# Causal row sums: added up on GpSimd over the key tiles, in place of float32r pairs of transposed probabilities

## The chip, the core and the metric

The kernel runs on one core of a Trainium2 chip, in one launch. A core has five engines with queues of their own: TensorE (PE in the profile; its weight loads are PEld), VectorE (DVE), ScalarE (ACT), GpSimd (POOL) and SyncE (SP), which here issues all DMAs. Each executes its queue strictly in order, and they wait for each other by semaphores. The metric is the device time of one execution in microseconds, the median over runs. Lower is better.

## The reference, cut to what matters

Four attention layers follow each other on an image of shape (4, 256, 32, 32): a batch of 4, C = 256 channels, N = 1024 pixels.

```python
# L0: full attention, 32 channels for queries and keys
attn = softmax(einsum('bnm,bmj->bnj', Q, K)); x = gamma * einsum('bcj,bij->bci', V, attn) + x
# L1 and L3: full attention over group-normed x, 256 channels
scores = einsum('bci,bcj->bij', q, k) * C ** -0.5
attn = softmax(scores, axis=2)
out = einsum('bcj,bij->bci', v, attn); x = x + conv1x1(out, wo, bo)
# L2: causal attention, 8 heads of 32, one shared key and value head, then a feed-forward block
sim = einsum('bhid,bjd->bhij', q, k); sim = where(causal, neg, sim)
out = einsum('bhij,bjd->bhid', softmax(sim), v)
```

Everything is float32. A softmax is a quotient: the exponentials times v, over the sum of the exponentials of a row.

## The kernel before, in words

**Twelve full layers.** L0, L1 and L3 for four batch elements each are twelve instances in the order of `FULL`. In each, scores of a query tile (128 queries, 1024 keys) are made by TensorE (`full_scores`), VectorE takes the maximum (`row_max`, L1442), ScalarE the exponentials and their sum (`exponents`, L1218), VectorE scales them by the inverse sum (`invert`, L1450), TensorE transposes them in two halves (`full_turn`, L888), and ScalarE copies these to `probsT` (`turned`, L1226). After four turns `full_values` multiplies a quarter of 256 queries by `vt`, for two halves of the channels (`ct`), over eight key tiles.

TensorE takes a float32 product in two instructions per tile. An operand can also be split in a rounded part `hi` and a rest `lo`, both float32r, and then a product is three instructions, one each: hi·hi, hi·lo, lo·hi (`product`, whose instructions have line L844). In `full_values` the first `PAIRED` = 3 key tiles go this way, the five others in float32 (L898). The splits of `probsT` and `vt` for those three are made by GpSimd (`pair`, L732 the cast, L734 the subtraction), which TensorE waits for (`probs_split`, `vt_split`).

**The causal layer.** L2 has per batch element eight blocks `k` (two head groups of four heads, times four query quarters `qi`), and a block has 2(qi+1) key tiles `jt`, its steps: 40 an element, 160 in all. A step is: TensorE makes the exponents' arguments (L1144), ScalarE the exponentials into one of three buffers of `cprobs` (L1371), GpSimd clears what is above the diagonal in a block's last two steps (L809, `diag_masked`), and two steps later (`LAG`) TensorE runs `causal_values` (L1163): for each of the four heads a product with v into columns 0 to 255 of the accumulator, and one with `ones` (all ones, 32 wide) into columns 256 to 511, which adds up the row sums. All are float32, in four column groups of the array side by side. A block's last step has 128 queries left, all others 256. VectorE then divides (`normalise`), and GpSimd splits the result (`heads_split`, L770 and L772) for the output product.

**Order.** Each engine weaves three chains, full (F), causal (C) and feed-forward (G), by a string in `ORDER` that says which chain is next; on TensorE the letters also give the PSUM bank of each unit. The strings are constants in the source. GpSimd also takes roots for the norms (`root`, L766 and L745) and writes normalised rows `an` (L779).

## Time and profile before

| | us |
|---|---|
| median of 3 runs (lowest, highest) | 1341.97 (1340.13, 1343.36) |
| the profiled execution | 1342.26 |
| its span, first to last instruction | 1340.4 |
| TensorE busy | 1261.6 |
| VectorE busy | 817.8 |
| ScalarE busy | 596.1 |
| GpSimd busy | 404.1 |

Busy time is the time in which an engine executes something. TensorE's matmuls are pipelined, and what one lasts reaches into the next, so what a matmul costs in the queue is the distance from its start to the next start. "Idle before" of a group is what its engine waited just ahead of it, with the one that released it. The chain of waits goes back from the last instruction to what released each.

### The profile page before, as it was taken

The page shows a single profiled execution, that of the slowest core. Times are in us where ns is not written, and L with a number is a line of the kernel's source. Part 1 is how long each engine was busy: PE and PEld are TensorE (multiplying, and loading weights), DVE is VectorE, ACT ScalarE, POOL GpSimd, SP SyncE. Part 2 cuts the span into 40 slices and gives each one's busy share as a digit, 9 for nine tenths or more (in the row PEclk, how much of TensorE's full clock was granted, in tenths as well). Part 3 has the DMA queues.
Part 4 walks back from the last instruction along what each step waited for, and adds up shares of the span by engine and source line. Part 5 has one row for each costly group of instructions (what it writes and reads, how often), then busy time and mean ns, then how long its engine had stood idle before and what let it go on. Part 6 is the DMA issues. An engine that isn't in the chain of part 4 may idle for free.

```text
span 1340.4 us, 22884 instructions
## 1 busy us (share of the span) xinstructions
PE 1261.6 (94%) x9088; PEld 1000.6 (75%) x9088; DVE 817.8 (61%) x1766; ACT 596.1 (44%) x1127; POOL 404.1 (30%) x478
## 2 busy tenths in 40 slices
PE   5979989999999899999999999989999999999797
PEld 5868877676778777767788777767787778668787
DVE  3644557677546857577567577575477575666342
ACT  3523443353554543534545345536435453553342
POOL 0212321322342433223323334323233243234222
PEclk9989999999999999999999999999999999999899
DMA  5000020100001010100020111000020101000000
GB/s 195 1 0 1 1 75 6 25 6 21 2 1 30 19 26 1 25 2 1 1 47 2 42 48 25 2 0 1 1 48 2 25 17 41 1 2 17 17 0 32
DMA packets 20618, 27.13 MB, mean 20 GB/s; under 512 B 3489, under 2 KB 14241, under 8 KB 20513
## 3 DMA queue, kind: packets, MB, share of 16 engines
q1 hardware_dynamic: 20512, 25.66, 6.9%
q8 instruction: 74, 1.21, 0.4%
q14 instruction: 32, 0.25, 0.1%
HBM read 8.61 MB, written 4.19 MB: 10 GB/s over the span
## 4 chain that ended last, share of the span: by engine, by line
PE 86%; DVE 7%; ACT 4%; issue 2%; POOL 1%; DMA 1%; SPq 0%; ACTq 0%; DVEq 0%
PE ring L844 36%; PE ring L898 16%; PE ring L1163 11%; PE ring L1144 6%; PE ring L1129 5%; PE ring L888 4%; PE ring L929 1%; ACT probs L1218 1%; PE ring L1063 1%; PE ring L1133 1%; PE ring L1098 1%; DVE shift_max L1442 1%; ACT probsT L1226 1%; DVE part_max L1735 1%; DVE neg_max L1439 1%
## 5 line engine op out<-in xcount | busy, mean ns | idle before, releaser
L1371 ACT ACTIVATE cprobs<-ring 128x512 f32<-128x512 f32 x288 | 164.7, 600 | 267.5 <-PE ring L1144 265.5
L898 PE MATMUL ring<-probsT,vt 128*128 128x256 f32 x960 | 227.6, 384 | 12.2 <-ACT probsT L1226 11.4
L898 PEld LDWEIGHTS ring<-probsT,vt 128*128 128x128 f32 x960 | 178.4, 192 | 40.4 <-ACT probsT L1226 15.5
L1218 ACT ACTIVATE probs<-ring,neg_max 128x1024 f32<-128x1024 f32 x96 | 106.9, 1114 | 161.0 <-DVE neg_max L1443 103.7
L732 POOL CAST probsT_hi<-probsT 128x384 fp32r<-128x384 f32 x96 | 65.2, 679 | 363.1 <-ACT probsT L1226 363.0
L1735 DVE TENSOR_REDUCE part_max<-ring 128x2 f32<-128x1024 f32 (+2 forms) x112 | 128.0, 1145 | 60.0 <-PE ring L1129 37.7
L1144 PE MATMUL ring<-qs,ks 98*128 98x512 f32 x288 | 124.9, 462 | 6.9 <-DMA qs<-max_rows 2.1
L1442 DVE TENSOR_REDUCE shift_max<-ring 128x1 f32<-128x1024 f32 x64 | 78.3, 1223 | 54.7 <-PE ring L844 50.6
L1226 ACT COPY probsT<-ring 128x512 f32<-128x512 f32 x192 | 101.9, 591 | 16.7 <-PE ring L888 16.7
L1129 PE MATMUL ring<-ks,qs 96*128 96x512 f32 (+3 forms) x384 | 103.5, 365 | 4.4 <-DVE part_max L1735 2.3
L888 PE MATMUL ring<-consts,probs 128*128 128x128 f32 x768 | 102.9, 274 | 4.8 <-DVE h_lo L1417 2.3
L844 PE MATMUL ring<-h_hi,q_hi 128*128 128x512 f32 x256 | 104.0, 406 | 0.2 <-issue 0.2
L734 POOL TENSOR_TENSOR probsT_lo<-probsT,probsT_hi 128x384 fp32r<-128x384 f32 x96 | 100.2, 1044 | 7.9
L888 PEld LDWEIGHTS ring<-consts,probs 128*128 128x128 f32 x768 | 88.2, 141 | 18.1 <-DVE h_lo L1417 3.1
L844 PE MATMUL ring<-h_hi,q_lo 128*128 128x512 f32 x256 | 100.4, 392 | 0.0
L844 PE MATMUL ring<-h_lo,q_hi 128*128 128x512 f32 x256 | 100.4, 392 | 0.0
L1163 PE MATMUL ring<-cprobs,v 128*32 128x256 f32 (+1 forms) x1280 | 96.4, 373 | 0.5 <-ACT gelu L1351 0.3
L1163 PE MATMUL ring<-cprobs,ones 128*32 128x256 f32 (+1 forms) x1280 | 92.3, 360 | 0.0
L844 PE MATMUL ring<-probsT_hi,vt_hi 128*128 128x256 f32 x288 | 91.5, 318 | 0.0
L1144 PEld LDWEIGHTS ring<-qs,ks 98*128 98x128 f32 x288 | 51.0, 190 | 48.1 <-issue 28.2
L844 PE MATMUL ring<-probsT_lo,vt_hi 128*128 128x256 f32 x288 | 81.1, 282 | 0.0
L844 PE MATMUL ring<-probsT_hi,vt_lo 128*128 128x256 f32 x288 | 81.1, 282 | 0.0
(238 smaller groups left out, 2643.0 us busy)
## 6 DMA issues: line engine op xcount, KB each, us to landing
qs<-q_hi SPq DMA_DIRECT2D x32, 128.0 KB, 2.4
qs<-q_hi SPq DMA_DIRECT2D x64, 64.0 KB, 2.0
x<-x_dram SPq DMA_DIRECT2D x3, 1024.0 KB, 7.4
qs<-q_lo SPq DMA_DIRECT2D x16, 128.0 KB, 2.3
qs<-max_rows SPq DMA_DIRECT2D x128, 2.0 KB
qs<-q_lo SPq DMA_DIRECT2D x32, 64.0 KB, 2.0
out_dram<-z SPq DMA_DIRECT2D x4, 512.0 KB, 2.8
out_dram<-x SPq DMA_DIRECT2D x4, 512.0 KB, 2.8
```

The costliest lines, as they stand in the source:

```text
L734: return pool.tensor_tensor(lo, src, hi.bitcast(F32), ALU.subtract)
L844: ins = mm(out, w, m, start=first and n == 0, stop=last and n == len(every) - 1)
L888: last = nc.tensor.transpose(o[:, j, :], probs[:, ti % 2, (TPH * hf + j) * P:(TPH * hf + j + 1) * P], ident)
L898: mm(own, vt[:, j, cs], probsT[:, qi % 2, j, :], start=j == PAIRED, stop=False)
L1129: last = mm(o, stack(k, a, 3 * DH, at, at + P), ks[0:3 * DH, lo:hi], start=i % own == 0, stop=not diag and i % own == own - 1)
L1144: mm(exponent_tiles(name, n), ks[0:3 * DH + 2, jt * P:(jt + 1) * P], stack(k, part_heads(part), 3 * DH + 2, QUARTER - n, QUARTER), start=T ...
L1163: last = mm(acc[DH * a:DH * (a + 1), (half + 1) * QUARTER - n:(half + 1) * QUARTER], w, causal_probs(step, n)[:, a, :], start=jt == 0 and ...
L1218: A(probs[:, ti % 2, :], flat(full_name(l, b, ("s", ti))), ACT.Exp, bias=neg_max[:, ti:ti + 1], accum_out=row_sum[:, ti:ti + 1]).then_inc( ...
L1226: nc.scalar.copy(probsT[:, ti // 2 % 2, js, (ti % 2) * P:(ti % 2 + 1) * P], slot(name)[:, 0, :].rearrange("p (s n) -> p s n", n=P)).then_i ...
L1371: A(causal_probs(step, n)[:, part_heads(part), :], exponent_tiles(name, n), ACT.Exp).then_inc(read_done[chain[name], "act"], 1)
L1442: full_then(v.tensor_reduce(shift_max[:, ti:ti + 1], flat(name), AX_X, ALU.max, negate=True))
L1735: v.tensor_reduce(cols if ti < TPH else parts[:, ch, :], src[:, :, 0:n], AX_X, ALU.max, negate=True).then_inc(read_done["c", "dve"], 1)
```

## The change

`PAIRED` and all that belongs to it go: `full_values` takes all eight key tiles in float32, and GpSimd no longer splits `probsT` and `vt`. In the causal layer, blocks with `qi` above 0 (`has_sum`) get their row sums in another way. GpSimd adds the probability tiles of a block elementwise into `block_sum` (one addition per key tile from the second on, 1024 elements a partition, 512 for the last), and TensorE multiplies that sum by `ones` once, at the block's last step, behind a wait for `summed`. ScalarE waits for `summed` before it overwrites a tile of `cprobs`. VectorE's `normalise` writes to buffers of its own and has the same operations. All strings in `ORDER` but SyncE's are new.

```diff
-PAIRED = 3
@@ ORDER (one line of many) @@
-        "FFFFFFFFFFFFFFFFFFCFFCFFFFFCCCCFFCCCCGGGFGCGCCFFCCGCGGFFCGFGCCFCFGGGCCCGGFFCCCCFGGGFGGFFCFCCFCFCFFCCCCFGGGFC"
+        "FCCCCCCCCCCCCCCGGGCCCCCGGCFCCCCCGCCCGCGCCCCCCCCCCGGCCCCGCCCGGCCCCCGCGCCCCCGGGGGCCCCCCCCCCCCGCGGCCCCCFCGGCCCC"
+def has_sum(k):
+    return BLOCKS[k][1] > 0
+
+def is_added(e):
+    return has_sum(e[1]) and e[2] >= 1 and e[4] > 0
@@ GpSimd @@
-                        pair(probsT_hi[at], probsT_lo[at], probsT[at],
-                             n * (NT + 1) + ti + 2).then_inc(probs_split, 1)
...
+            def add(b, e):
+                _, k, jt, step, _ = e
+                n = queries(k, jt)
+                total = block_sum[:, k % 2, :, QUARTER - n:QUARTER]
+                if e in diagonal:
+                    pool.wait_ge(diag_masked, b * DIAG + diagonal.index(e) + 1)
+                else:
+                    wait_read(pool, causal_name(b, e))
+                if jt == 1:
+                    if b or has_sum(k - 2):
+                        wait_filled(pool, f"C{b}.o{k - 2}" if has_sum(k - 2) else f"C{b - 1}.o{k + K - 4}")
+                    first = causal_probs(step - 1, n)
+                else:
+                    pool.wait_ge(summed, b * ADDED + added.index(e))
+                    first = total
+                pool.tensor_tensor(total, first, causal_probs(step, n), ALU.add).then_inc(summed, 1)
@@ TensorE, full_values @@
-                    for j in range(PAIRED, NT):
-                        mm(own, vt[:, j, cs], probsT[:, qi % 2, j, :], start=j == PAIRED, stop=False)
-                    yield
-                    if ct == 0:
-                        pe.wait_ge(vt_split, n + 1)
-                        pe.wait_ge(probs_split, n * NT + 2 * qi + 2)
-                    last = product(own, [([w[:, j, cs] for w in (vt_hi, vt_lo)],
-                                          [p[:, qi % 2, j, :] for p in (probsT_hi, probsT_lo)]) for j in range(PAIRED)],
-                                   first=False)
...
+                    for j in range(NT):
+                        last = mm(o[:, ct * QUARTER:(ct + 1) * QUARTER], vt[:, j, ct * P:(ct + 1) * P],
+                                  probsT[:, qi % 2, j, :], start=j == 0, stop=j == NT - 1)
...
@@ TensorE, causal_values @@
-                for half, w in ((0, v2[:, jt, :]), (1, ones[:, 0:DH])):
-                    for a in range(4):
-                        last = mm(acc[DH * a:DH * (a + 1), (half + 1) * QUARTER - n:(half + 1) * QUARTER], w,
-                                  causal_probs(step, n)[:, a, :], start=jt == 0 and half == 0, stop=is_final(e) and half == 1)
+                for a in range(4):
+                    mm(acc[DH * a:DH * (a + 1), QUARTER - n:QUARTER], v2[:, jt, :], causal_probs(step, n)[:, a, :],
+                       start=jt == 0, stop=False)
+                if has_sum(k):
+                    if not is_final(e):
+                        return
+                    pe.wait_ge(summed, b * ADDED + added_no(exp))
+                    tiles, n = block_sum[:, k % 2, :, :], QUARTER
+                else:
+                    tiles = causal_probs(step, n)
+                for a in range(4):
+                    last = mm(acc[DH * a:DH * (a + 1), 2 * QUARTER - n:2 * QUARTER], ones[:, 0:DH], tiles[:, a, :],
+                              start=False, stop=is_final(e))
@@ ScalarE, causal exponents @@
+                        if step < STEPS:
+                            if b:
+                                act.wait_ge(summed, b * ADDED)
+                        elif has_sum(probabilities[step - STEPS][1]):
+                            act.wait_ge(summed, b * ADDED + added_no(probabilities[step - STEPS]))
```

TensorE's queue before, one half of a value product of the first full layer (`probsT` by `vt` in float32, then `hi` and `lo` parts):

```order
99 L898 MATMUL ring<-probsT,vt 128x256 x5
100 L844 MATMUL ring<-probsT_hi,vt_hi 128x256
101 L844 MATMUL ring<-probsT_lo,vt_hi 128x256
102 L844 MATMUL ring<-probsT_hi,vt_lo 128x256
103 L844 MATMUL ring<-probsT_hi,vt_hi 128x256
```

The same engine in the changed kernel. The row with x16 holds both halves:

```order
88 L904 MATMUL ring<-consts,probs 128x128 x8
89 L891 MATMUL ring<-ks_57,qs_56 128x512 x2
90 L904 MATMUL ring<-consts,probs 128x128 x8
91 L913 MATMUL ring<-probsT,vt 128x256 x16
92 L891 MATMUL ring<-ks_57,qs_56 128x512 x2
```

The five float32 tiles and nine float32r instructions of a half have become eight float32 tiles.

TensorE's queue before, in block 6 of the last batch element (`cprobs` by `v` and by `ones`, between arguments of exponents `qs` by `ks`); row 3908 is the block's last:

```order
3898 L1163 MATMUL ring<-cprobs,v_144 32x256 x4
3899 L1163 MATMUL ring<-cprobs,ones 32x256 x4
3900 L1144 MATMUL ring<-qs,ks 128x512
3901 L1163 MATMUL ring<-cprobs,v_144 32x256 x4
3902 L1163 MATMUL ring<-cprobs,ones 32x256 x4
3903 L1144 MATMUL ring<-qs,ks 128x512 x2
3904 L1163 MATMUL ring<-cprobs,v_144 32x256 x4
3905 L1163 MATMUL ring<-cprobs,ones 32x256 x4
3906 L1144 MATMUL ring<-qs,ks 128x512 x2
3907 L1163 MATMUL ring<-cprobs,v_144 32x128 x4
3908 L1163 MATMUL ring<-cprobs,ones 32x128 x4
```

The same place in the changed kernel; row 3084 is the block's one product with ones:

```order
3078 L1154 MATMUL ring<-qs,ks 128x512 x2
3079 L913 MATMUL ring<-probsT,vt 128x256 x4
3080 L1172 MATMUL ring<-cprobs,v_141 32x256 x4
3081 L1154 MATMUL ring<-qs,ks 128x512 x2
3082 L913 MATMUL ring<-probsT,vt 128x256 x8
3083 L1172 MATMUL ring<-cprobs,v_141 32x128 x4
3084 L1182 MATMUL ring<-block_sum,ones 32x256 x4
3085 L1073 MATMUL ring<-consts,an 128x128 x4
3086 L1154 MATMUL ring<-qs,ks 128x512 x2
3087 L1172 MATMUL ring<-cprobs,v_141 32x256 x4
```

The ones product behind every v product is gone, and other work stands between the steps.

GpSimd's queue before, at that block (masks of `cprobs`, splits, roots, rows of `an`):

```order
378 L766 TENSOR_TENSOR rstd_g<-var_eps_g,half_neg 128x2
379 L732 CAST probsT_hi<-probsT 128x3x128
380 L734 TENSOR_TENSOR probsT_lo<-probsT,probsT_hi 128x3x128
381 L809 AFFINE_SELECT cprobs<-cprobs 128x4x128 x2
382 L766 TENSOR_TENSOR rstd_g<-var_eps_g,half_neg 128x2
383 L779 TENSOR_SCALAR an<-xs,ln_mv_g,rstd_g 128x256 x2
384 L770 CAST heads_out_hi<-nums 128x256
385 L772 TENSOR_TENSOR heads_out_lo<-nums,heads_out_hi 128x256
```

The changed kernel, from the block's first addition to its last:

```order
292 L808 TENSOR_TENSOR block_sum<-cprobs 128x1024
293 L808 TENSOR_TENSOR block_sum<-block_sum,cprobs 128x1024
294 L765 CAST heads_out_hi<-nums 128x256
295 L767 TENSOR_TENSOR heads_out_lo<-nums,heads_out_hi 128x256
296 L808 TENSOR_TENSOR block_sum<-block_sum,cprobs 128x1024 x3
297 L761 TENSOR_TENSOR rstd_g<-var_eps_g,half_neg 128x2
298 L822 AFFINE_SELECT cprobs<-cprobs 128x4x128
299 L808 TENSOR_TENSOR block_sum<-block_sum,cprobs 128x1024
300 L761 TENSOR_TENSOR rstd_g<-var_eps_g,half_neg 128x2
301 L822 AFFINE_SELECT cprobs<-cprobs 128x4x128
302 L774 TENSOR_SCALAR an<-xs,ln_mv_g,rstd_g 128x256 x2
303 L808 TENSOR_TENSOR block_sum<-block_sum,cprobs 128x4x128
```

Seven additions stand where two masks stood, in one chain with the splits of `heads_out`, the roots and the rows of `an`.

## Rows read from the trace of the kernel before

**Rows 1.** Page, busy time of each engine over the span.

```profile
PE 1261.6 (94%) x9088; PEld 1000.6 (75%) x9088; DVE 817.8 (61%) x1766; ACT 596.1 (44%) x1127; POOL 404.1 (30%) x478
```

**Rows 2.** Windows: us, busy us of PE, PEld, DVE, ACT, POOL, clock, DMA, GB/s.

```profile
0.00:200.00 200.00, 167.23 (x966) 146.31 (x967) 97.27 (x197) 79.07 (x153) 45.33 (x53) 0.97 0.15 45
200.00:1200.00 1000.00, 968.99 (x7331) 746.44 (x7329) 663.10 (x1442) 468.70 (x882) 320.41 (x382) 0.99 0.06 16
1200.00:1340.40 140.40, 125.35 (x794) 107.87 (x793) 57.47 (x127) 48.36 (x93) 38.34 (x43) 0.98 0.04 16
```

**Rows 3.** Timeline of TensorE, causal steps around 374 us: start, us, what.

```profile
373.74 0.64 PE L1163 MATMUL ring<-cprobs,v 128*32 128x256 f32 x8
374.19 0.61 PE L1163 MATMUL ring<-cprobs,ones 128*32 128x256 f32 x8
374.74 0.73 PE L1144 MATMUL ring<-qs,ks 98*128 98x512 f32 x2
375.40 0.64 PE L1163 MATMUL ring<-cprobs,v 128*32 128x256 f32 x8
```

**Rows 4.** Timeline of TensorE, a narrow causal step.

```profile
351.71 0.42 PE L1163 MATMUL ring<-cprobs,v 128*32 128x128 f32 x8
351.95 0.40 PE L1163 MATMUL ring<-cprobs,ones 128*32 128x128 f32 x8
```

**Rows 5.** Chain of waits, pieces around 1308 us: start, us, what.

```profile
1308.29 2.16 PE ring L898 x10
1310.45 1.07 PE ring L844 x9
```

**Rows 6.** Page, costliest groups of TensorE.

```profile
L898 PE MATMUL ring<-probsT,vt 128*128 128x256 f32 x960 | 227.6, 384 | 12.2 <-ACT probsT L1226 11.4
```

**Rows 7.** Groups by shape, GpSimd: busy us, mean ns, idle before.

```profile
L734 POOL TENSOR_TENSOR probsT_lo<-probsT,probsT_hi 128x384 fp32r<-128x384 f32 x96 | 100.2, 1044 | 7.9
L732 POOL CAST probsT_hi<-probsT 128x384 fp32r<-128x384 f32 x96 | 65.2, 679 | 363.1 <-ACT probsT L1226 363.0
L809 POOL TENSOR_SCALAR_AFFINE_SELECT cprobs<-cprobs 128x512 f32<-128x512 f32 x64 | 41.0, 645 | 89.6 <-ACT cprobs L1371 89.5
L779 POOL TENSOR_SCALAR an<-xs,ln_mv_g,rstd_g 128x256 f32<-128x256 f32 x32 | 40.4, 1270 | 1.7 <-POOL rstd_g L766 0.5
L766 POOL TENSOR_TENSOR rstd_g<-var_eps_g,half_neg 128x2 f32<-128x2 f32 x48 | 37.5, 782 | 131.2 <-DVE var_eps_g L1629 130.9
L772 POOL TENSOR_TENSOR heads_out_lo<-nums,heads_out_hi 128x256 fp32r<-128x256 f32 x32 | 23.5, 734 | 2.7
L734 POOL TENSOR_TENSOR vt_lo<-vt,vt_hi 128x768 fp32r<-128x768 f32 x12 | 22.3, 1856 | 1.0
L770 POOL CAST heads_out_hi<-nums 128x256 fp32r<-128x256 f32 x32 | 13.2, 411 | 147.8 <-DVE nums L1764 147.8
```

**Rows 8.** Chain of waits, pieces of GpSimd around 179 and 1240 us.

```profile
178.14 0.83 POOL vt_hi L732
179.04 1.85 POOL vt_lo L734
180.90 1.42 POOL rstd_c L766
...
1240.16 1.00 POOL probsT_lo L734
```

**Rows 9.** Page, ScalarE's causal exponents.

```profile
L1371 ACT ACTIVATE cprobs<-ring 128x512 f32<-128x512 f32 x288 | 164.7, 600 | 267.5 <-PE ring L1144 265.5
```

**Rows 10.** Chain of waits, a run of float32r products of 512 columns.

```profile
102.30 5.21 PE ring L844 x23
```

**Rows 11.** VectorE's scaling of probs: one instance in the timeline, all 96, and their group.

```profile
179.29 2.16 DVE L1450 TENSOR_SCALAR probs<-probs,row_inv 128x1024 f32<-128x1024 f32 x1
...
L1450 DVE TENSOR_SCALAR probs<-probs,row_inv x96: 752/754/2160, 33.3 to 1320.5; 128x1024 f32<-128x1024 f32 x96
...
L1450 DVE TENSOR_SCALAR probs<-probs,row_inv 128x1024 f32<-128x1024 f32 x96 | 77.3, 805 | 3.4
```

More of the change, by code:

```diff
@@ L79 @@
+        "GCCCGCCFCCCCCCGGGGGCCCCCCCCCCCCCGGGCCCGCGCFCCCCGCCCGCGGGCCCCCCCCCCCCCCGCCGCGCCCCCGCGCCCCCCGGGGGF"),
     "SP": (
@@ L397, in build @@
     DIAG = len(diagonal)
+    probabilities = [e for e in schedule if e[0] == "exp" and e[4]]
+    added = [e for e in probabilities if is_added(e)]
+    ADDED = len(added)
     last_max = {e[1]: e for e in schedule if e[0] == "max"}
@@ L447, in build @@
         ks0 = shared("ks0", [P, N], r_g + 4 * KIB, F32R)
-        vt, vt_lo = (shared(n, [P, NT, C], r_v, d) for n, d in (("vt", F32), ("vt_lo", F32R)))
-        vt_hi = shared("vt_hi", [P, PAIRED, C], r_v + 8 * KIB, F32R)
+        vt = shared("vt", [P, NT, C], r_v)
         probs = shared("probs", [P, 2, N], r_p)
         h_full = shared("h_full", [P, CT, N], r_h + 8 * KIB)
-        probsT, probsT_lo = (shared(n, [P, 2, NT, QUARTER], r_t, d) for n, d in (("probsT", F32), ("probsT_lo", F32R)))
-        probsT_hi = shared("probsT_hi", [P, 2, PAIRED, QUARTER], r_t + 16 * KIB, F32R)
+        probsT = shared("probsT", [P, 2, NT, QUARTER], r_t)
         def gn_stats(l, b):
@@ L465, in build @@
         cprobs = shared("cprobs", [P, STEPS, 4, QUARTER], r_c)
+        block_sum = shared("block_sum", [P, 2, 4, QUARTER], r_b)
         qs = shared("qs", [P, HG, 4, 2 * QUARTER], r_s, F32R)
@@ L564, in build @@
         diag_masked = sem("diag_masked")
[L565 removed]
+        summed = sem("summed")
         split_step = sem("split_step")
@@ L653, in qk_product, with added_no @@
             return slot(f"prep.qk{l[1]}")[:, 0, :].rearrange("p (c o) -> p c o", o=C)
+        def added_no(e):
+            return 1 + next(i for i, f in enumerate(added) if f[1] == e[1] and f[2] >= e[2])
         def stack_done(eng, b, k):
@@ L729, in _ @@
             pool.wait_ge(setup, 2)
[L731 to L756 removed]
+            def full_chain():
+                n = 0
+                for l, b in FULL:
+                    if l == "L0":
+                        continue
+                    n += 1
+                    pool.wait_ge(gn_var_ready, n)
+                    pool.tensor_tensor(gn_rstd[:, :], gn_var[:, :], half_neg[:, 0:CT], ALU.pow).then_inc(gn_rstd_ready, 1)
                     yield
@@ L805, in causal_chain @@
                         yield
[L806 to L811 removed]
+                    elif e[0] == "exp":
+                        if e in diagonal:
+                            wait_read(pool, causal_name(b, e))
+                            d = causal_probs(e[3], P)
+                            pool.affine_select(out=d, in_=d, pattern=[[0, 4], [1, P]], compare_op=ALU.is_ge,
+                                               fill=0.0, base=0, channel_multiplier=-1).then_inc(diag_masked, 1)
+                            yield
+                        if is_added(e):
+                            add(b, e)
+                            yield
             def feed_chain():
@@ L983, in full_chain @@
                     else:
-                        yield from full_values(l, b, n, e[1])
+                        yield from full_values(l, b, e[1])
                         continue
```

117 lines of the change are left out of this document (44 added, 73 removed).

## The prediction

> **What bounds the kernel now.** I read the busy times first: TensorE works 1261.6 us of a span of 1340.4, VectorE 61%, ScalarE 44%, GpSimd 30% [rows 1]. Then the stretches: between 200 and 1200 us, where the causal layer runs woven with the full ones, TensorE is busy 969 of 1000 us, and GpSimd only 320 [rows 2]. So nearly all of the time is the sum of what TensorE has to do, plus 79 us of idle (1340.4 - 1261.6), of which 33 lie before 200 us, 31 in the middle and 15 behind 1200. An edit that takes work out of TensorE's queue in the middle should come back nearly whole; one that adds work there costs its full length. The working is made against the profiled execution, 1342.3 us with its span of 1340.4; the median of the runs is 1342.0, the same within 0.02%.
>
> **Part 1: products with ones go.** In each key step of the causal layer TensorE multiplies the probabilities by v (four column groups, two passes each: 8 instructions) and then by ones (8 more). What an instruction lasts in the timeline (0.64 and 0.61 us for these groups) overlaps its neighbours, so I go from start to start: v at 373.74, ones at 374.19, the next at 374.74; v again at 375.40 [rows 3]. A group of 256 columns holds the queue for 0.46 us. The ones group seems to hold it for 0.55, but the extra 0.09 comes behind whichever such group is last, and v stays, so it isn't saved. A group of 128 columns costs 0.24 us (351.71 to 351.95) [rows 4]. Per batch element there are 40 steps: 36 in the six blocks with query quarter above 0, six of them (each block's last) narrow, and 4 in the two first blocks, which keep what they have. The six blocks lose 30 wide and 6 narrow ones groups and get one wide group each: 24 wide and 6 narrow fewer. Over four elements 96 x 0.46 + 24 x 0.24 = 44.2 + 5.8 = 50.0 us less.
>
> **Part 2: three of eight key tiles go back to float32.** The full layers' value product took 5 tiles in float32 and 3 as float32r pairs. In the chain of waits ten float32 instructions (5 tiles) take 2.16 us and the nine float32r ones 1.07 us, and this pair of rows comes again for every output half [rows 5]. Three tiles in float32 are 6 x 0.216 = 1.30 us, so a half costs 1.30 - 1.07 = 0.22 us more. 12 layers x 4 query quarters x 2 halves = 96 halves (the 960 instructions of the float32 group over ten [rows 6]): 96 x 0.223 = 21.4 us more. This is TensorE work with no cover. So the pairs did help, and giving them up takes back almost half of part 1.
>
> **Part 3: what GpSimd gives up.** The splits of probsT cost it 65.2 + 100.2 us and those of vt_lo 22.3 [rows 7]; the casts to vt_hi go too. Most of that was under TensorE's work, but at two places the chain of waits runs through it: vt_hi and vt_lo at 178.14 to 180.90 (0.83 + 1.85 us), ahead of a root that VectorE's normalisation waited for, and probsT_lo at 1240.16 (1.00 us) ahead of the rows that TensorE waited for [rows 8]. What comes late next there is the root itself (1.42 us). I take 3 us off, with 0 and 4 as its ends.
>
> **Part 4: what GpSimd gets.** 3, 5 and 7 additions in the blocks of query quarter 1, 2 and 3, two blocks each: 30 per element, 120 in all, 24 of them (the last of a block) of 512 elements a partition and 96 of 1024. No row shows a tensor_tensor of 1024 elements. Of the same engine, with two float32 inputs, 384 elements take 1.044 us, 768 take 1.856 and 256 take 0.734 [rows 7]: 0.0021 us an element and 0.2 fixed, so 2.40 us for 1024 and 1.28 for 512 (an estimate from these rows). From below, 1024 cannot be under the 1.86 us that 768 take; from above, four of the 256 form in a row would be 2.94. I take 2.40, since the three rows lie on one line. Total 96 x 2.40 + 24 x 1.28 = 261 us, so GpSimd goes from 404 to at most 404 - 188 + 261 = 477 us, 36% of the span: no bound on average.
>
> The question is whether a single addition is waited for. Two new waits exist. ScalarE may not overwrite one of three probability tiles before its addition is done, and behind its waiting exponent stand the copies of probsT and the next exponents. TensorE waits at each block's ones product, and all its queue stands behind. I laid the queues side by side at the place where the additions lie closest, block 6 of the last element, printed in the section on the change. GpSimd has 6 wide additions and a narrow one between, with two masks, one pair of heads_out, two roots and two rows of `an`: 14.4 + 1.3 + 1.3 + 1.1 + 1.6 + 2.5 = 22.2 us [rows 7], and some 0.08 us between any two of the 14, so 23.3, and 0.9 for the first exponent (0.60 us [rows 9]) and the hops. TensorE's queue between that exponent's product and the wait holds 12 float32 value tiles (5.2 us), 35 float32r products of 512 columns at 0.227 (5.21 us for 23 [rows 10]; 7.9), 12 of 256 (1.4), 7 wide and 2 narrow v groups (3.7), and 16 transpose passes, masks and small products (some 3.3, an estimate), together 21.5, and about 0.3 us at each of the 9 v groups for going in and out (0.66 us between 374.74 and 375.40 for two products of 0.227, and the 0.09 above [rows 3]), so 24.2 us. Equal within the error: up to 3 us late there. Summing the same way for the other 23 blocks, only four further places come out late, by under 1 us each except for the third tile in the block behind (up to 5 us); the least TensorE work between a block's last exponent and its ones product is 5.4 us, against 0.6 + 0.64 + 1.28 us for exponent, mask and narrow addition. So I book 6 us for new waits, bounds 0 and 17 (the latter if each wide addition took 3.0 us).
>
> A GpSimd operation also holds VectorE back: the scaling of probs took 2.16 us at 179.29 against a median of 0.754, and began while vt_lo ran (179.04 for 1.85 us) [rows 8, 11]. Over its 96 instances the mean is 0.805 [rows 11], so all of this costs 96 x 0.051 = 5 us of VectorE's time today. The chance to meet an operation and the wait behind it both grow with its length, so I scale by count times length squared: about 371 now, 766 after. The 5 us become 10, a few more for the operations that read two tiles, on an engine that is busy 61%. That is inside the 6 us.
> The Trainium skill (SBUF — State Buffer, section "SBUF: two separate sides") says that VectorE and GpSimd share one port pair as an exclusive lock, and that the loser blocks for the whole instruction. The row above agrees: 179.04 + 1.85 = 180.89, and the scaling ended at 181.45. By that rule the longest locks grow from 1.0 (1.9 for vt_lo) to 2.4 us, and the rule speaks against this change: if every sum came 0.6 us late by it, the time would be 1331 in place of 1317.
>
> **The sum.** 1342.3 - 50.0 + 21.4 - 3 + 6 = 1316.7, so 1317 us, 1.9% faster. All waits and the rate of TensorE's clock (0.99 mean [rows 2]) are otherwise taken as before. Its own range, from the ends above, is 1309 to 1327.
>
> **Rivals.**
> 1. The order comes out better as well. The orders of four engines are written anew, and 31 us of TensorE's idle time in the middle leave room. For it: the densest eight causal steps held 13.3 us of TensorE work before, against 17.9 now, so bursts are spread. Against: the order before already had 97% busy there. If a third of the 31 and a few of the end's 15 go, 1317 - 13 = 1304.
> 2. The gain is half swallowed: additions and locks delay VectorE's scaling and ScalarE's exponents, and TensorE's freed 28.6 us come back in part as idle time. For it: the blocks of the last element have no slack (part 4), and 24 ones products are new waits. Against: GpSimd's share of 36%, 5.4 us of cover at the tightest end. At 0.6 us late for each of 24 ones products, 14 us: 1331.
> 3. Slower: the addition in place. If a wide one holds its place for 3.6 us or more (2.4 of its own and 1.2 of VectorE's operations ahead of it, or a slower form), the 6 in a block such as that above run 7.2 us over a place with no slack, and the three tiles pass it on to ScalarE, whose probsT copies TensorE needs. It decides from the point where the 24 blocks are late by 1.3 us on average (31.6 us in all: 50.0 - 21.4 + 3). I price it at 1.65 us late each: 1342.3 - 50.0 + 21.4 - 3 + 39.6 = 1350. Against it: the rows of 384 to 768 elements hardly scatter from one line [rows 7].
>
> **Chances.** Forecast 0.60, rival 1 0.15, rival 2 0.18, rival 3 0.05, and 0.02 for no change. A measurement of this kernel can tell about 0.2% (2.7 us) from no change. Faster 0.91, same 0.03, slower 0.06. The range holds the forecast and most of rivals 1 and 2: 1301 to 1335.
>
> **What would show it.** TensorE's busy time should be near 1261.6 - 28.6 = 1233 us. The ones rows should count 320 instructions, the float32 value product 1536, at 2.16 us per ten. GpSimd's wide additions should have a mean of 2.4 to 2.5 us. TensorE's idle time should be 80 to 85 us, with a few us behind block_sum. The forecast is wrong if ScalarE's exponents wait tens of us for block_sum and TensorE for probsT behind them, if the wide additions lie above 3 us, if a ones group saved less than 0.46 us, or if VectorE's scaling has a mean far above 0.85 us.

## The result and the profile after

The changed kernel takes 1358.5 us (three runs, 1357.39 to 1360.69) against 1341.97: a ratio of 1.0128 with an interval of 1.0110 to 1.0146, so 1.3% slower. The forecast was 1317 us, faster. The profiled execution took 1360.69 us with a span of 1358.9.

The page of the changed kernel, busy time of each engine, and the shares of the chain that ended last:

```profile
PE 1255.7 (92%) x7840; PEld 985.2 (73%) x7840; DVE 888.8 (65%) x1766; ACT 598.8 (44%) x1127; POOL 468.7 (34%) x382
...
PE 70%; DVE 20%; issue 4%; ACT 4%; POOL 1%; DMA 0%; SPq 0%; ACTq 0%; DVEq 0%
```

TensorE has 1248 instructions fewer than in [rows 1] and is only 6 us less busy; its idle time grew from 79 to 103 us. VectorE has the same 1766 instructions and is 71 us busier. In the chain of the kernel before the shares were:

```profile
PE 86%; DVE 7%; ACT 4%; issue 2%; POOL 1%; DMA 1%; SPq 0%; ACTq 0%; DVEq 0%
```

TensorE's fell from 86 to 70% and VectorE's rose from 7 to 20%, while GpSimd, which got the new work, has 1% as before. So neither GpSimd's load nor its sums are what mostly ends late; it is VectorE.

The same three stretches as in [rows 2] (us, busy us of TensorE, its loads, VectorE, ScalarE, GpSimd, then clock, DMA, GB/s):

```profile
0.00:200.00 200.00, 171.62 (x924) 149.22 (x925) 94.77 (x198) 79.25 (x153) 3.07 (x9) 0.97 0.15 46
200.00:1200.00 1000.00, 943.28 (x6127) 720.39 (x6125) 726.98 (x1426) 463.83 (x868) 425.27 (x341) 0.98 0.06 15
1200.00:1358.90 158.90, 140.82 (x792) 115.63 (x791) 67.04 (x143) 55.69 (x107) 40.33 (x33) 0.95 0.04 14
```

In the middle TensorE's idle time went from 31 to 57 us, and VectorE's busy time from 663 to 727.

The additions by shape, and TensorE's groups that answer to [rows 4 to 6] (busy us, mean ns, idle before):

```profile
L808 POOL TENSOR_TENSOR block_sum<-block_sum,cprobs 128x1024 f32<-128x1024 f32 x72 | 172.6, 2397 | 70.5 <-ACT cprobs L1395 67.6
L808 POOL TENSOR_TENSOR block_sum<-cprobs 128x1024 f32<-128x1024 f32 x24 | 57.4, 2391 | 80.8 <-ACT cprobs L1395 80.8
...
L808 POOL TENSOR_TENSOR block_sum<-block_sum,cprobs 128x512 f32<-128x512 f32 x24 | 30.9, 1289 | 1.7
```

```profile
L913 PE MATMUL ring<-probsT,vt 128*128 128x256 f32 x1536 | 358.3, 385 | 14.3 <-ACT probsT L1245 13.7 <-ACT gelu L1370 0.6
...
L1182 PE MATMUL ring<-block_sum,ones 128*32 128x256 f32 x192 | 15.2, 390 | 1.7 <-POOL block_sum L808 1.7
...
L1182 PE MATMUL ring<-cprobs,ones 128*32 128x256 f32 x64 | 4.9, 379 | 0.0
...
L1182 PE MATMUL ring<-cprobs,ones 128*32 128x128 f32 x64 | 3.2, 273 | 0.0
```

The additions take 2.39 and 1.29 us, TensorE waits for them 1.7 us in all, and there are 320 products with ones. This is as forecast. Now VectorE's groups by shape, after, and then the same forms before (the scaling of `probs` stands in [rows 11]):

```profile
L1474 DVE TENSOR_SCALAR probs<-probs,row_inv 128x1024 f32<-128x1024 f32 x96 | 81.8, 852 | 3.4
...
L1674 DVE SCALAR_TENSOR_TENSOR xs<-xs,rstd_g,rows 128x256 f32<-128x256 f32 x32 | 26.5, 870 | 0.1
...
L1763 DVE TENSOR_TENSOR cmax<-part_max 128x2 f32<-128x2 f32 x32 | 25.3, 790 | 1.1
...
L1467 DVE SCALAR_TENSOR_TENSOR neg_max<-shift_max,key_bias 128x1 f32<-128x1 f32 x64 | 23.2, 362 | 2.3
...
L1653 DVE TENSOR_SCALAR var_eps_g<-ln_mv_g 128x2 f32<-128x2 f32 x48 | 19.1, 397 | 1.7
```

```profile
L1650 DVE SCALAR_TENSOR_TENSOR xs<-xs,rstd_g,rows 128x256 f32<-128x256 f32 x32 | 16.6, 559 | 3.4 <-POOL rstd_g L766 3.4
...
L1443 DVE SCALAR_TENSOR_TENSOR neg_max<-shift_max,key_bias 128x1 f32<-128x1 f32 x64 | 15.6, 244 | 2.3
...
L1629 DVE TENSOR_SCALAR var_eps_g<-ln_mv_g 128x2 f32<-128x2 f32 x48 | 8.8, 184 | 1.7
...
L1739 DVE TENSOR_TENSOR cmax<-part_max 128x2 f32<-128x2 f32 x32 | 6.4, 200 | 1.1
```

An operation on two numbers a partition (`cmax`) went from a mean of 200 to 790 ns. The scaling of `probs`, the one group on which the prediction looked for this, went from 805 to 852 only. The timeline of VectorE and then of GpSimd around 1181 us shows what happens (start, us, what):

```profile
1181.47 2.37 DVE L1763 TENSOR_TENSOR cmax<-part_max 128x2 f32<-128x2 f32 x1
```

```profile
1181.44 2.38 POOL L808 TENSOR_TENSOR block_sum<-cprobs 128x1024 f32<-128x1024 f32 x1 [6.33 <-ACT cprobs L1395]
```

`cmax` started 0.03 us behind an addition and ended with it: 2.37 us for work of 0.16. Through the whole trace, 16 of the 48 `cmax` operations started while an addition ran; they took 1.5 us more than 0.16 on average, with 1.7 us of the addition still to run. The 25 that started while GpSimd did nothing took 0.16.

A second place shows how that reaches TensorE, and what the clock adds. VectorE, GpSimd, and TensorE around 796 us:

```profile
795.25 1.93 DVE L1763 TENSOR_TENSOR cmax<-part_max 128x4 f32<-128x4 f32 x1
797.10 2.34 DVE L1759 TENSOR_REDUCE part_max<-ring 128x2 f32<-128x1024 f32 x2
```

```profile
794.79 2.37 POOL L808 TENSOR_TENSOR block_sum<-cprobs 128x1024 f32<-128x1024 f32 x1 [0.42 <-ACT cprobs L1395]
```

```profile
796.08 0.40 PE L1154 MATMUL ring<-qs,ks 98*128 98x512 f32 x1
798.37 1.17 PE L1139 MATMUL ring<-ks,qs 96*128 96x256 f32 x4 [1.89 <-DVE part_max L1759]
799.34 0.65 PE L1143 MATMUL ring<-mask 128*128 128x128 bf16 x4
799.92 1.08 PE L1172 MATMUL ring<-cprobs,v 128*32 128x256 f32 x8
```

`cmax` is held until the addition's end at 797.16 (794.79 + 2.37), the maxima behind it start that much later, and TensorE, which needs a PSUM place they read, idles 1.89 us. In stretches of 4 us (columns as above, the last but two is the granted clock):

```profile
796.00:800.00 4.00, 2.11 (x15) 1.38 (x17) 3.80 (x4) 1.00 (x2) 4.00 (x4) 0.81 0.15 58
800.00:804.00 4.00, 4.00 (x21) 3.01 (x22) 3.17 (x8) 2.21 (x3) 2.30 (x3) 0.50 0.00 0
804.00:808.00 4.00, 4.00 (x31) 2.14 (x29) 3.24 (x4) 3.98 (x6) 0.72 (x1) 0.84 0.00 0
```

After a stretch in which TensorE worked only 2.11 of 4 us the clock is at 0.50, the 1.2 GHz level: the group of eight `v` products takes 1.08 us in place of the 0.64 of [rows 3]. Such falls are seen before too, but there are more of them in this execution: a mean granted clock of 0.990 over the span before is some 27 us at that level, one of 0.975 here is some 68 us (an estimate from the two clocks and spans, with two levels only). The two other executions of the changed kernel had 0.982 and 0.986.

### The profile page after: what moved, and what is told of

Same layout as the page of the kernel before. It is cut to its first block, busy times and chain, and to the rows that moved or that the text cites. A ratio compares the mean times of both kernels' runs of the same rounds, so it can differ in the third digit from the quotient of the medians.

```text
span 1358.9 us, 20604 instructions
## 1 busy us (share of the span) xinstructions
PE 1255.7 (92%) x7840; PEld 985.2 (73%) x7840; DVE 888.8 (65%) x1766; ACT 598.8 (44%) x1127; POOL 468.7 (34%) x382
## 3 DMA queue, kind: packets, MB, share of 16 engines
q8 instruction: 64, 1.05, 0.3%
## 4 chain that ended last, share of the span: by engine, by line
PE 70%; DVE 20%; issue 4%; ACT 4%; POOL 1%; DMA 0%; SPq 0%; ACTq 0%; DVEq 0%
PE ring L860 24%; PE ring L913 22%; PE ring L1154 4%; DVE part_max L1759 4%; PE ring L1172 4%; PE ring L1139 4%; PE ring L904 3%; DVE cmax L1763 2%; DVE shift_max L1466 2%; ACT probs L1237 1%; PE ring L939 1%; ACT probsT L1245 1%; DVE xs L1674 1%; PE ring L1108 1%; PE ring L1073 1%
## 5 line engine op out<-in xcount | busy, mean ns | idle before, releaser
L913 PE MATMUL ring<-probsT,vt 128*128 128x256 f32 x1536 | 358.3, 385 | 14.3 <-ACT probsT L1245 13.7
L913 PEld LDWEIGHTS ring<-probsT,vt 128*128 128x128 f32 x1536 | 290.9, 192 | 61.8 <-ACT probsT L1245 17.2
L808 POOL TENSOR_TENSOR block_sum<-block_sum,cprobs 128x1024 f32<-128x1024 f32 x96 | 203.5, 2120 | 72.2 <-ACT cprobs L1395 67.6
L1139 PE MATMUL ring<-ks,qs 96*128 96x512 f32 (+3 forms) x384 | 107.3, 375 | 17.3 <-DVE part_max L1759 11.2
L860 PE MATMUL ring<-h_hi,q_hi 128*128 128x512 f32 x256 | 106.9, 418 | 3.3 <-DVE q_lo L1443 2.6
L1139 PEld LDWEIGHTS ring<-ks,qs 96*128 96x128 f32 x384 | 63.0, 194 | 38.2 <-DVE part_max L1759 16.8
L822 POOL TENSOR_SCALAR_AFFINE_SELECT cprobs<-cprobs 128x512 f32<-128x512 f32 x64 | 43.1, 673 | 129.3 <-ACT cprobs L1395 129.3
L761 POOL TENSOR_TENSOR rstd_g<-var_eps_g,half_neg 128x2 f32<-128x2 f32 x48 | 37.1, 773 | 141.9 <-DVE var_eps_g L1653 141.0
L808 POOL TENSOR_TENSOR block_sum<-cprobs 128x1024 f32<-128x1024 f32 x24 | 57.4, 2391 | 80.8 <-ACT cprobs L1395 80.8
L1474 DVE TENSOR_SCALAR probs<-probs,row_inv 128x1024 f32<-128x1024 f32 x96 | 81.8, 852 | 3.4
```

The source lines that it names most:

```text
L808: pool.tensor_tensor(total, first, causal_probs(step, n), ALU.add).then_inc(summed, 1)
L860: ins = mm(out, w, m, start=first and n == 0, stop=last and n == len(every) - 1)
L913: last = mm(o[:, ct * QUARTER:(ct + 1) * QUARTER], vt[:, j, ct * P:(ct + 1) * P], probsT[:, qi % 2, j, :], start=j == 0, stop=j == NT - 1)
L1139: last = mm(o, stack(k, a, 3 * DH, at, at + P), ks[0:3 * DH, lo:hi], start=i % own == 0, stop=not diag and i % own == own - 1)
```

## The experiments

Theory A: two-source operations of VectorE (and its copies) are held by a running addition on GpSimd, and by them the causal chain comes late. Rivals: GpSimd's own queue and late sums (B), and that parts 1 and 2 of the prediction were mispriced. The kernel before took 1342.1 to 1343.3 us (medians) beside these runs.

**1. One-column additions.**

```diff
+            pool.memset(block_sum[:, :, :, :], 1.0)
-                pool.tensor_tensor(total, first, causal_probs(step, n), ALU.add).then_inc(summed, 1)
+                pool.tensor_tensor(total[:, :, 0:1], first[:, :, 0:1], causal_probs(step, n)[:, :, 0:1], ALU.add).then_inc(summed, 1)
```

> The changed kernel, but each of GpSimd's 120 additions takes one column per head (4 elements a partition in place of 1024 or 512), into a block_sum set to 1 at the start: the row sums are left out, while order, waits and TensorE's work are the changed kernel's. Theory A (the additions' length is what costs: they hold VectorE's operations and their waiters): VectorE's busy time falls from 889 us to about 815, TensorE's idle time from 103 to about 80, and the time is about 1317 us. Rival B (the new order, or the float32 work, costs): over 1340 us, with VectorE back at 815 and nothing won. Rival C (only the clock differs): 1340 to 1350 with the idle time as in the changed kernel.

Measured 1316.66 us, ratio 0.9813 (0.9790 to 0.9835). Instructions, order and waits are those of the changed kernel; only the additions' length differs, and it is worth 42 us, as theory A had it. TensorE's and VectorE's busy times and the chain:

```profile
PE 1239.0 (94%) x7840; PEld 978.1 (74%) x7840; DVE 803.2 (61%) x1766; ACT 598.1 (45%) x1127; POOL 235.6 (18%) x383
...
PE 81%; DVE 10%; ACT 4%; issue 2%; SPq 1%; DMA 1%; POOL 1%; ACTq 0%; DVEq 0%; POOLq 0%
```

The 42.6 us between the spans of the two profiled executions are 16.7 us of TensorE's busy time (1255.7 - 1239.0 for the same 7840 instructions, at a mean clock of 0.975 and 0.985) and 25.9 of idle time (103.2 - 77.3). Of the latter the waits for VectorE alone give 15.8 us (35.9 to 51.7 over all lines of the view of waits), those for GpSimd 2.3. The line of that view that fell most, after and then with one-column additions (waited for: us in total, times, longest):

```profile
PE ring L1139 <- DVE part_max L1759: 11.2, 10, 1.9
```

```profile
PE ring L1140 <- DVE part_max L1760: 4.7, 7, 1.1
```

**2. Part 2 alone.** The kernel before with all eight value tiles in float32 and no splits of `probsT` and `vt` on GpSimd.

```diff
-                    for j in range(PAIRED, NT):
-                        mm(own, vt[:, j, cs], probsT[:, qi % 2, j, :], start=j == PAIRED, stop=False)
...
+                    for j in range(NT):
```

> The kernel before with part 2 alone: all eight key tiles in float32, no splits by GpSimd, everything else and every engine's order as before. By the prediction's term TensorE has 21.4 us more and GpSimd's places on the chain give 3 back: 1342 + 21 - 3 = 1360 us. Rival: the splits held VectorE and GpSimd enough that giving them up pays for most of it: 1345 to 1350 us. A second rival: float32 work costs more than its columns (it changes TensorE's clock or waits): over 1368 us.

1362.08 us, ratio 1.0150 (1.0124 to 1.0176): 20.0 us more, where the prediction's parts 2 and 3 had 21.4 - 3 = 18.4.

**3. Part 1 alone, without a sum.** One ones group at each block's end in place of six or so, nothing added up; the float32r pairs stay.

```diff
+                if summing and not is_final(e):
+                    return
```

> The kernel before without 30 wide and 6 narrow ones groups per element; each of the six blocks takes one ones group over constants at its end, so the row sums are left out. float32r pairs and order stay, and nothing is added on GpSimd. By the prediction's term of 0.46 and 0.24 us a group: 1342 - 50 = 1292 us. Rival (the groups covered waits of the other engines, so half comes back as idle time): 1310 to 1320 us, with TensorE's busy time at 1212 and its idle time over 95.

1303.42 us, ratio 0.9718 (0.9690 to 0.9747): 38.7 us less, not 50.0, so some 11 us of part 1 did not come on the old order of work. In the profiled executions TensorE's busy time fell by 43.6 us (1261.6 to 1218.0, at a mean clock of 0.990 and 0.987) and its idle time grew by 3.0 (78.9 to 81.9): the larger part of what is missing is busy time, not waiting.

**4. Both, on the old order.** Experiments 2 and 3 in one kernel.

> The kernel before, in its own order, with the 36 products with ones per element replaced by one group at each of the six blocks' ends and with all eight value tiles in float32; no additions, no float32r splits on GpSimd. Left out: the sum over key tiles. If parts 1 and 2 add up on this order (38.7 us less and 20.1 us more, measured apart) it takes 1321 to 1326. Rival: if part 1's 11 us were lost to GpSimd's splits, 1310 to 1316, no slower than the changed kernel with one-column additions (1316.7); a time above 1320 says that the changed order of work itself is worth 5 us or so.

1319.79 us, ratio 0.9816 (0.9788 to 0.9844). The sum of the two apart is 1323.6. The changed order with one-column additions (1316.66) is 3 us better than this, which their intervals don't separate. The new order is not to blame.

**5. Shorter pieces.** Each wide addition as two of 512 columns, then as four of 256.

```diff
+                for i in range(n // P):
+                    half = slice(2 * i, 2 * i + 2) if n > P else slice(0, 4)
+                    ins = pool.tensor_tensor(total[:, half, :], first[:, half, :], probs_here[:, half, :], ALU.add)
```

> The changed kernel with each wide addition as two of 512 elements. GpSimd's busy time rises by 96 x 0.17 = 16 us, and the longest hold halves. If what costs is how long one instruction holds VectorE's operations (theory A): VectorE's busy time falls from 889 to about 850 us and the time to about 1345. Rival (GpSimd's own queue is what is waited for): no faster than 1358, and up to 1365.

> The changed kernel with each wide addition issued as four of 256 columns (narrow ones as two). By the narrow and the half addition one takes about 0.73 us, four 2.9. Theory A: what is lost goes with how long a single addition holds, so it falls further than with two halves (which gave 8 us): 1338 to 1347, the cmax group's mean below 350 ns. Rival B (GpSimd's queue): the additions are 50 us longer in all, so 1355 to 1370.

1350.61 us (1.0063, interval 1.0040 to 1.0086) and 1343.92 us (1.0002, interval 0.9987 to 1.0017): 8 and 15 us off the changed kernel, though GpSimd is 19 and 56 us busier (487.3, 525.1). B would have had it slower. The rest doesn't go: the 27 us that four pieces still lose come with a larger part of GpSimd in the chain (4% in place of 1%), and waits of TensorE for GpSimd grew from 4.2 to 9.1 us. So pieces seem to trade holding for queueing; how the 27 us divide between the two wasn't measured.

**6. Another form of the held operation.**

```diff
-                    ins = v.tensor_tensor(cols, parts[:, 0, :], parts[:, 1, :], ALU.min)
+                    ins = v.tensor_reduce(cols, parts.rearrange("p c h -> p h c"), AX_X, ALU.min)
```

> The changed kernel with one VectorE operation in another form: the smallest of the two halves' maxima (cmax<-part_max, 48 instructions of 2 or 4 elements) is taken by a reduction over one source instead of an operation with two sources. Theory A (VectorE operations that need both sources from SBUF, or copy in their quick form, wait until the running addition on GpSimd ends): the 48 go from 32.5 us to about 9, VectorE busy 865, time 1346 to 1353. Rival B (the sums arrive late or queue on GpSimd, VectorE is not what costs): 1356 to 1361. Rival C (every VectorE operation on SBUF is held, whatever its form): the reductions take as long as the pair operation did, 0.7 to 0.8 us each, and the time stays at 1357 to 1360.

1349.2 us, ratio 1.0042 (1.0021 to 1.0063): 9 us back for 48 operations of two or four numbers each, inside theory A's range. Rival C falls: the reduction never waits. The group, and next to it the cast behind it, which now comes earlier and is held instead:

```profile
L1768 DVE CAST cmax_hi<-cmax 128x8 fp32r<-128x8 f32 x32 | 11.5, 359 | 1.1
...
L1763 DVE TENSOR_REDUCE cmax<-part_max 128x2 f32<-128x4 f32 x32 | 5.0, 158 | 1.1
```

In the timeline of this kernel, VectorE and GpSimd at 614 us, the cast is held from start to end by an addition, at the moment after the reduction:

```profile
613.93 0.16 DVE L1763 TENSOR_REDUCE cmax<-part_max 128x2 f32<-128x4 f32 x1
614.12 2.38 DVE L1768 CAST cmax_hi<-cmax 128x8 fp32r<-128x8 f32 x1
```

```profile
614.12 2.36 POOL L808 TENSOR_TENSOR block_sum<-block_sum,cprobs 128x1024 f32<-128x1024 f32 x1 [2.71 <-ACT cprobs L1395]
```

All 15 reductions that started under an addition took 0.16 us, with 1.6 us of it left on average.

**7. GpSimd's time without the flow of data.** Ten additions of one column per head for each wide one.

```diff
+                for i in range(10 if n > P else 5):
+                    ins = pool.tensor_tensor(total[:, :, i:i + 1], first[:, :, i:i + 1], probs_here[:, :, i:i + 1], ALU.add)
```

> The changed kernel with each wide addition replaced by ten additions of one column per head (220 ns each in the one-column kernel, so about 2.2 us of GpSimd; narrow ones by five); the other columns' sums are left out. GpSimd's time and the moment at which each sum is ready stay as in the changed kernel, while only 1/25 of the data flows. If the holding of VectorE by the flow of data costs the 42 us: 1317 to 1325, cmax mean below 300 ns. If GpSimd's queue and late sums cost them, or the hold lasts as long as instructions run whatever they move: 1340 to 1358; in the second case the cmax mean is above 500 ns, in the first below 300.

1315.69 us, ratio 0.9807 (0.9769 to 0.9845), `cmax` at 179 ns. The ten ran closer together than assumed (1.6 to 1.8 us for ten, 188.5 us in all, 72% of the full additions), so B isn't tested to its end, but nothing of the 42 us is left. At 1039.85 ten of them start; `cmax` under them took 0.25 us:

```profile
1039.85 1.79 POOL L811 TENSOR_TENSOR block_sum<-cprobs 128x4 f32<-128x4 f32 x10 [5.23 <-ACT cprobs L1399]
```

```profile
1041.09 0.25 DVE L1767 TENSOR_TENSOR cmax<-part_max 128x4 f32<-128x4 f32 x1
```

**8. One source in place of two.** Each addition replaced by a copy, then by a multiplication by 1.0; no sum.

```diff
+                pool.tensor_copy(total, causal_probs(step, n)).then_inc(summed, 1)
...
+                pool.tensor_scalar(total, causal_probs(step, n), 1.0, None, ALU.mult).then_inc(summed, 1)
```

> The changed kernel with each addition replaced by a copy of the step's tile into the same sum buffer (one source instead of two; the sum is left out). By the casts of 256 and 384 columns in the trace a copy of 1024 is about 1.7 to 2.1 us, against 2.40. Theory A with the hold by running time: 20 to 35 of the 42 us remain, 1337 to 1352, cmax mean 500 to 700 ns. Rival D (only a GpSimd operation with two sources holds VectorE): cmax mean below 250 ns, 1315 to 1323 as with the one-column additions.

> The changed kernel with each addition replaced by a multiplication of the step's tile by 1.0 into the sum buffer: one source, no sum. How long it takes on GpSimd the trace doesn't show for these operands (a copy took 1.05 us, a shift and scale with two per-row numbers 1.24 for 256 columns); 1.1 to 2.4 us is assumed. If it takes over 2 us and the form doesn't matter: 1345 to 1360. If only two sources hold: below 1325 at any length. If it takes about 1.1 us it repeats the copy: 1316 to 1320.

The copy takes 1.05 us and the kernel 1318.41 us, ratio 0.9823 (0.9787 to 0.9860); `cmax` mean 328 ns, above theory D's bound, so a copy holds as well, only briefly. The multiplication is the telling one:

```profile
L809 POOL TENSOR_SCALAR block_sum<-cprobs 128x1024 f32<-128x1024 f32 x96 | 269.9, 2811 | 123.6 <-ACT cprobs L1396 120.1 <-POOL block_sum L809 1.4
...
L809 POOL TENSOR_SCALAR block_sum<-cprobs 128x512 f32<-128x512 f32 x24 | 37.9, 1577 | 1.8
```

It keeps GpSimd 47 us longer than the additions did, and each lasts 0.4 us longer, yet the kernel takes 1327.83 us, ratio 0.9884 (0.9856 to 0.9912): 31 us less than with additions. GpSimd's queue is later than it was: ScalarE's exponents wait 18.5 us for `block_sum` in place of 8.8, TensorE 6.9 us for GpSimd in place of 4.2. So rival B can't be what cost these 31 us. Of the 11 us that remain over one-column additions a part may be B's queue, as GpSimd has 7% of the chain; that part wasn't measured. Here `cmax` and the multiplication start together, at 830.8:

```profile
830.85 1.03 DVE L1764 TENSOR_TENSOR cmax<-part_max 128x2 f32<-128x2 f32 x1
```

```profile
830.83 2.78 POOL L809 TENSOR_SCALAR block_sum<-cprobs 128x1024 f32<-128x1024 f32 x1 [14.07 <-ACT cprobs L1396]
```

That is the longest of the 17 `cmax` operations that started under one: 0.87 us of holding, a third of its length. The mean holding of the 17 is 0.27 us, with 1.8 us left to run; under additions it was 1.5. The trace tells when the holding ends. The seven that were held had all started within 0.65 us of the multiplication's start, and all ended 1.05 us after that start, which is what the copy takes in all; the ten that started later took 0.16. VectorE's copies and its scalings with one source can be held a second time, in the last microsecond of the multiplication:

```profile
879.33 0.98 DVE L1770 COPY max_cols<-cmax_hi 128x8 f32<-128x8 f32 x1
```

```profile
877.51 2.77 POOL L809 TENSOR_SCALAR block_sum<-cprobs 128x1024 f32<-128x1024 f32 x1 [0.15 <-POOL block_sum L809]
```

The copy started 0.95 us before the multiplication's end and ended with it. Both expectations were half right: the multiplication doesn't hold two-source operations to its end, but it does hold them.

**9. Half the columns, or half the number.** Additions over two of four heads; then every second addition in full, the others over one column.

```diff
+                pool.tensor_tensor(total[:, 0:2, :], first[:, 0:2, :], causal_probs(step, n)[:, 0:2, :], ALU.add).then_inc(summed, 1)
...
+                m = n if added.index(e) % 2 == 0 else 1
```

> The changed kernel with each addition over two of the four heads only (the sums of the other two are left out: the buffer holds ones). A wide one then takes about 1.29 us, all together some 141 us of GpSimd, next to 116 us of the copies that cost 2 us over the one-column additions and 261 us of the full additions that cost 42. Theory F (what is lost depends on the form: an addition with two sources holds VectorE, a copy hardly): about half of the 42 us is lost, 1334 to 1342, cmax mean 400 to 550 ns. Theory G (it depends on GpSimd's busy time only, and below some 120 us it fits into gaps): 1317 to 1325, cmax mean 250 to 350 ns like the copy's.

> The changed kernel with every second addition over all columns and the others over one column per head (sums left out), so 130 us of full-length additions plus 13 of short ones, against 141 us at half length that cost 5 us. If what matters is the length of one instruction (a hold of up to 2.4 us outlasts the slack that one of 1.29 us fits into): 1334 to 1342. If what matters is GpSimd's total: 1319 to 1326, as at half length.

1321.77 us (0.9847, interval 0.9828 to 0.9866) for 141 us of additions at half length, 1329.29 us (0.9900, interval 0.9872 to 0.9928) for 130 us at full length, so 5 and 13 us of the 42. The second lies between its two expectations. Length matters (the second is slower with less work), and the loss grows faster than the amount: half of either costs less than a third. In the first run the time is theory G's, and the `cmax` mean (351 ns) lies at the upper end of G's range, below F's. But G, which looks at GpSimd's total alone, doesn't explain why the second is slower.

**10. The best complete version.** Additions in four or two pieces, and three small steps as reductions; the same steps in the kernel before.

```diff
-                    causal_then(v.tensor_copy(cmax_hi[:, s, :, :], cmax[:, s, :, :]))
+                    causal_then(v.tensor_reduce(cmax_hi[:, s, :, :], cmax[:, s, :, :].unsqueeze(3), AX_X, ALU.max))
```

> The changed kernel, complete, with the additions in four pieces and three small VectorE steps of the causal maxima (cmax, cmax_hi, the even columns of max_cols) taken as reductions, the form that was not held. Four pieces gave 15 us, the first reduction alone 9 to 10, and some of it came back as a held cmax_hi cast (171 to 359 ns), which now goes as well. If the two add up: 1330 to 1337, faster than the kernel before. If they remove the same waits: 1337 to 1343, no change against before. Rival (GpSimd's string of pieces is what is late by now): 1342 to 1346.

> As the last, with the additions in two pieces (8 us by themselves). GpSimd is 38 us less busy than with four. If what is late is GpSimd's string: as fast as four pieces or faster, 1332 to 1340. If it is the length of one hold: 5 to 7 us slower than four pieces, 1338 to 1345.

> The kernel before with the same three small steps as reductions, for a fair comparison with the two above. There cmax takes 200 and 163 ns, the cast 178, the copy 182, against about 160 in the unheld form: 3 us of VectorE in all, off the path. So 1339 to 1343, no change. If the reductions were a gain of their own whatever GpSimd does: 1332 to 1337.

1340.8 us, ratio 0.9992 (0.9975 to 1.0010); 1343.74 us, 1.0016 (1.0000 to 1.0033); and before with reductions 1342.09 us, 1.0000 (0.9986 to 1.0015). Four pieces with reductions win back 18 us of the 42 and end level with the kernel before, no faster. So the two remedies don't add up: together they give little more than four pieces alone (1343.92). Two pieces are 3 us slower than four, where one theory had them as fast or faster and the other 5 to 7 us slower. What is still lost is 24 us over one-column additions. Candidates are other held operations, which kept their forms (means with one-column additions and here: `neg_max` 227 and 340 ns, `xs` 498 and 658, `var_eps_g` 170 and 236), and GpSimd's queue, 6% of that kernel's chain; no run separates them.

## Why the prediction was wrong

**Right.** Part 4's additions: 2.40 and 1.28 us forecast, 2.39 and 1.29 measured; GpSimd at most 477 us busy, measured 468.7. The new waits proper: 1.7 us of TensorE, 8.8 us of ScalarE's exponents for `block_sum`, for 6 us booked with bounds of 0 and 17. Part 2 with part 3: 18.4 forecast, 20.0 measured (experiment 2). The counts, 320 and 1536.

**Off in size.** Part 1 counted 50.0 us and by itself gave 38.7 (experiment 3), where TensorE's busy time fell by 43.6 and 3.0 came back as idle time: the price of a ones group was about an eighth too high in busy time, of which a part may be the slightly lower clock (0.987 against 0.990). The sum still meets the kernel with one-column additions (1316.7 forecast, 1316.66 measured), but as two errors that cancel. Without its 6 us for waits, which that kernel hardly has, the forecast was 31.6 us less (50.0 - 18.4); measured together it was 25.4 and apart 18.7 (38.7 - 20.0). On the old order, experiment 4 measured 22.5 us together (1342.3 - 1319.8), which lies between the last two; neither step of the 7 us is clear of the intervals, so what makes them stays open. The upper end of the sum's own range is also off: with all its ends it adds up to 1331 (1342.3 - 50.0 + 21.4 - 0 + 17), not 1327, which is still far below what was measured.

**The step that failed.** Part 4's last: "The 5 us become 10, a few more for the operations that read two tiles [...] That is inside the 6 us." VectorE's busy time is 85.6 us above that of one-column additions (888.8 - 803.2), and the kernel takes 42 us more. Three things were wrong in it. It priced the holding from one group, the scaling of `probs`. For that group the scaling rule came out: 5 us before (96 x 0.051), 9 after (96 x 0.098, the mean of 852 ns over the same 754), though only 7 of its 96 instances start under an addition. But that group has 8 of the 85.6 us (81.8 - 73.7), and `cmax` alone has 24 (32.5 - 8.4), `xs` 12 and `var_eps_g` 11. It didn't look at the small two-source steps of the causal chain: 16 of the 48 `cmax` operations start under an addition, and 0.16 us of work can become 2.37. And it took 61% of busy time on VectorE as room, while TensorE's next scores wait for just those maxima: the cover was an average, the chain is not.

The rule of the Trainium skill (SBUF — State Buffer, section "SBUF: two separate sides"), that the loser blocks for the whole instruction, was quoted and speaks exactly of this; the pairs at 1181 and 614 us agree (held 2.2 of 2.4 us). The prediction weighed it as 1331 at 0.6 us for each of 24 sums, that is, it looked for the damage at the sums. The multiplication of experiment 8 doesn't agree with "the whole instruction": it held `cmax` for 0.87 of 2.78 us at most, and let it go 1.05 us after its own start each time.

**The rivals.** Rival 2 named the mechanism ("additions and locks delay VectorE's scaling and ScalarE's exponents") and priced it at 14 us, a third of its size. Rival 3 had the sign and nearly the time, 1350, for another reason: the additions do not hold their place for 3.6 us, so its nearness is luck. Rival 1 isn't borne out: the old order without the additions is within 3 us of the new.

**The clock** was "taken as before". In the profiled pair TensorE is 16.7 us longer busy at the lower clock, and pauses behind VectorE are followed by stretches at the 1.2 GHz level, as at 796 us. But these 16.7 us are not what the clock cost: another execution of the changed kernel had a mean clock of 0.986, no lower than the 0.985 of the profiled execution with one-column additions, and took 1357.39 us against 1318.08. So 39 of the 42 us stand without a lower clock, and over the three executions 0.975 and 0.986 differ by 3.3 us. That the pauses bring the falls is read from such rows alone; no run sets the clock by itself.

**What would have shown it wrong.** Of the signs that were named, TensorE's busy time (1233 forecast, 1255.7) and its idle time (80 to 85, measured 103) showed it; of the four that were tied to a mechanism, three did not (exponents behind `block_sum` 8.8 us, additions 2.39, the scaling 0.852). The fourth, a ones group that saves less than 0.46 us, did come true in experiment 3 (38.7 of 50.0), but its 11 us are not the 42. None of them looked at a small operation.

## What to carry to other kernels

Before work is moved to GpSimd, list VectorE's small steps with two SBUF sources, its copies and its one-source scalings that stand in a chain TensorE waits for: each can be stretched to the end of one GpSimd addition, however small it is, and VectorE's and GpSimd's average load say nothing of it. What counts is how long one addition flows and how many of those steps start under it; a reduction with one source in place of a two-source step cost nothing here and wasn't held, and a one-source operation on GpSimd held two-source steps far less than an addition of about the same length. Price a second-order wait from the shortest operations in the chain, not from the largest group.

## What the runs showed of the hardware

- VectorE's operations with two SBUF sources, and its casts, copies and one-source scalings, were held until the running two-source addition on GpSimd ended (`cmax` 0.16 to 2.37 us, a cast 0.17 to 2.38, the scaling of `probs` 0.75 to 2.57). Not held were reductions from SBUF (0.16 us in each of 15 cases), reductions from PSUM (1.22 us each before and after), and a product with one of its two sources in PSUM (`nums`, 0.42 us in each of 8 cases).
- GpSimd's one-source multiplication of 1024 columns (2.8 us) held two-source operations only until 1.05 us after its start, so for 0.87 us at most, and a copy and some one-source scalings also in its last microsecond, to its end. Its copy (1.05 us) held `cmax` for 0.84 us at most, ten additions of four elements in 1.8 us for 0.09.
- On GpSimd a copy of 1024 float32 columns took 1.05 us, an addition of two tiles 2.39, and a multiplication by a constant 2.81: it has fewer sources than the addition and is slower.
- The loss isn't linear in the additions' total: 130 to 141 us of them cost 5 to 13 us, 261 us cost 42.
